# Two slots for filler work instead of one in a fused attention and feed-forward kernel

## The reference

```python
xn = layernorm(x)                      # x: (2, 8192, 1024)
latent = xn @ Wc_down                  # 1024 -> 512
q = latent @ Wq_up                     # 16 heads of 64
k, v = split(latent @ Wkv_up)          # one k, one v of 64 for all heads
y = softmax(causal(q k^T / 8)) v
s = y @ Wc_proj
gate = xn @ (w_gate/127).T; up = xn @ (w_up/127).T     # 1024 -> 3072
ffn = (silu(gate) * up) @ (w_down/127).T
out = x + s * silu(ffn)
```

## Time and profile before

| | us |
|---|---|
| median of the runs (2 runs, 3533.99 to 3546.13) | 3540.06 |
| the profiled execution | 3540.48 |
| its span, slowest core (core 0) | 3538.0 |
| spans of the other seven cores | 3485.8 to 3526.6 |
| TensorE busy | 2251.4 (64%) |
| ScalarE busy | 1336.4 (38%) |
| VectorE busy | 1189.5 (34%) |
| GpSimd busy | 413.1 (12%) |

### The profile page before, as it was taken

The page is one execution under the profiler, slowest core; times in us unless marked ns, Lnnn a source line. Parts: engine busy times, 40 slices in busy tenths (PEclk is TensorE's granted clock), DMA queues, the critical chain, the costliest instruction groups (busy, mean ns, idle before and its releaser), DMA issues.

```text
span 3538.0 us, 34007 instructions; the slowest of 8 cores (3485.8 to 3538.0 us)
## 1 busy us (share of the span) xinstructions
PE 2251.4 (64%) x10552; PEld 1056.5 (30%) x10592; DVE 1189.5 (34%) x2154; ACT 1336.4 (38%) x1489; POOL 413.1 (12%) x329
## 2 busy tenths in 40 slices
PE   1334546455574685584757748598576798488886
PEld 1212223222241252252224322252222442223422
DVE  3545342432423334424243241422322321411221
ACT  0112222221331343232534437344455436375355
POOL 0100212123042100100000000000000000000000
PEclk7556767676696796796869968677676787687878
DMA  5000539548193271461006300063000251011500
GB/s 94 32 33 32 66 63 120 92 78 154 23 110 73 36 169 51 104 153 65 32 14 134 112 21 25 14 150 96 14 17 26 65 141 43 15 31 45 141 26 13
DMA packets 549452, 240.57 MB, mean 68 GB/s; under 512 B 476576, under 2 KB 532896, under 8 KB 549280
## 3 DMA queue, kind: packets, MB, share of 16 engines
q1 hardware_dynamic: 431952, 195.27, 20.9%
q0 software_dynamic: 117328, 43.14, 11.3%
HBM read 250.00 MB, written 27.26 MB: 78 GB/s over the span
## 4 chain that ended last, share of the span: by engine, by line
PE 39%; DVE 20%; DMA 16%; issue 11%; ACT 10%; POOL 4%; DVEq 1%; SPq 0%; ACTq 0%; POOLq 0%
PE ps_y L548 10%; PE ps_sc L561 9%; ACT p_sb L572 7%; PE ps_u L717 5%; PE ps_u L724 4%; PE ps_u L788 3%; POOL p_sb L580 3%; DVE recbf L600 3%; DMA wd_t<-wdbf 3%; DMA wu_t<-wu 3%; PE ps_u L638 2%; DVE stat L299 2%; DMA wd_t<-wd 2%; DMA xt<-xb 2%; DVE xnT L371 2%
## 5 line engine op out<-in xcount | busy, mean ns | idle before, releaser
L572 ACT ACTIVATE p_sb<-ps_sc 128x1024 bf16<-128x1024 f32 x1088 | 1099.9, 1023 | 1483.0 <-PE ps_sc L561 1465.9
L548 PE MATMUL ps_y<-p_sb,vaug_sb 128*65 128x512 bf16 x2176 | 773.2, 442 | 236.9 <-POOL p_sb L580 147.3
L561 PE MATMUL ps_sc<-qs,kT_sb 65*128 65x512 bf16 x2176 | 774.3, 443 | 20.0 <-DVE qs L529 20.0
L580 POOL TENSOR_TENSOR p_sb<-p_sb,masks_sb 128x1024 bf16<-128x1024 bf16 x128 | 273.1, 2143 | 2698.2 <-ACT p_sb L572 2698.0
L548 PEld LDWEIGHTS ps_y<-p_sb,vaug_sb 128*65 128x65 bf16 x2176 | 218.7, 123 | 693.6 <-issue 628.7
L788 PE MATMUL ps_u<-wd_t,h_sb 128*128 128x512 bf16 x744 | 234.6, 444 | 140.7 <-DMA wd_t<-wd 59.0
L561 PEld LDWEIGHTS ps_sc<-qs,kT_sb 65*128 65x128 bf16 x2176 | 227.2, 110 | 245.8 <-issue 138.2
L717 PE MATMUL ps_u<-xnT_own,wg_t 128*128 128x256 bf16 x1536 | 228.3, 299 | 97.5 <-DVE h_sb L735 55.1
L590 DVE CAST yf<-ps_y 64x1024 bf16<-64x1024 f32 x32 | 38.8, 1213 | 617.7 <-PE ps_y L548 617.7
L364 PE MATMUL ps_u<-ident_sb,xn_t 128*128 128x128 bf16 x640 | 81.0, 269 | 259.5 <-DVE xn_t L329 225.7
L724 PE MATMUL ps_u<-xnT_own,wu_t 128*128 128x256 bf16 x1536 | 229.3, 299 | 21.5 <-DMA wu_t<-wu 21.3
(11 more groups left out here) (88 smaller groups left out, 1391.7 us busy)
## 6 DMA issues: line engine op xcount, KB each, us to landing
wg_t<-wgbf SPq DMA_DIRECT2D x144, 256.0 KB, 3.5
wu_t<-wubf SPq DMA_DIRECT2D x144, 256.0 KB, 3.7
wd_t<-wdbf SPq DMA_DIRECT2D x288, 128.0 KB, 2.2
xt<-xb SPq DMA_DIRECT2D x64, 512.0 KB, 4.6
xo_t<-xo SPq DMA_DIRECT2D x32, 512.0 KB, 3.9
wg_t<-wg POOLq DMA_DIRECT2D x48, 256.0 KB, 9.0
wu_t<-wu POOLq DMA_DIRECT2D x48, 256.0 KB, 8.9
wd_t<-wd POOLq DMA_DIRECT2D x96, 128.0 KB, 3.9
```

Source lines behind the costliest of these rows:

```text
L548: last = O("tensor", lambda e_, t=t, nh=nh, par=par: e_.matmul(ps_y[0:65, nh * 512:(nh + 1) * 512], vaug_sb[:, t, :], p_sb[:, par, nh * 51 ...
L561: sct = O("tensor", lambda e_, t=t, nh=nh, sb2=sb2: e_.matmul(ps_sc[:, sb2 * 1024 + nh * 512:sb2 * 1024 + (nh + 1) * 512], kT_sb[0:65, t * ...
L572: ex = O("scalar", lambda e_, sb2=sb2: e_.activation(p_sb[:, sb2, :], ps_sc[:, sb2 * 1024:(sb2 + 1) * 1024], AF.Exp), [sct, st["p_war"][sb ...
L580: mtoks[t] = O("gpsimd", lambda e_, pview=pview, mj=mj: e_.tensor_tensor(pview, pview, masks_sb[:, mj, :].unsqueeze(1).broadcast_to([128, ...
```

## The change

The one variable becomes two: act_m for a must or epilogue generator, act_l for a lazy one. A pump first goes on with act_m. If there is none, it advances lazy work when nothing of tq_must or of the ready epiq is pending, and also at every third pump when something is. Only then does it start an entry of tq_must or epiq. So a feed-forward piece stands at every third pump between must generators, though never inside one, and ready epilogues come ahead of lazy work. A lazy generator that stalls uses its pump up.

The core of the diff (the two draining loops after it replace `park_or_finish` by `finish_must` and active by act_l in the same manner):

```diff
--- before.py
+++ after.py
@@ -851,7 +851,8 @@
         tq_must = deque()
         tq_lazy = deque()
         epiq = deque()
-        active = [None]
+        act_m = [None]
+        act_l = [None]
         tick = [0]
         EPI_DELAY = 6
 
@@ -875,40 +876,38 @@
                     return "stall"
             return "active"
 
-        def start_item(item, lazy=False):
-            r = item()
-            if r is None:
-                return
-            if adv(r, 1, tq_lazy) == "active":
-                active[0] = (r, lazy)
-
-        def park_or_finish():
-            a = active[0]
-            if a is None:
-                return
-            if a[1]:
-                tq_lazy.appendleft(a[0])
-            else:
-                for _ in a[0]:
+        def finish_must():
+            if act_m[0] is not None:
+                for _ in act_m[0]:
                     pass
-            active[0] = None
-
-        def lazy_step_force():
-            a = active[0]
-            if a is not None and a[1]:
-                if adv(a[0], 1, tq_lazy) != "active":
-                    active[0] = None
-                return
+                act_m[0] = None
+
+        def lazy_step():
+            if act_l[0] is not None:
+                r = adv(act_l[0], LAZY_STEPS)
+                if r == "stall":
+                    tq_lazy.appendleft(act_l[0])
+                    act_l[0] = None
+                elif r == "done":
+                    act_l[0] = None
+                return True
             if tq_lazy:
                 ent = tq_lazy.popleft()
                 if callable(ent):
                     ent = ent()
                     if ent is None:
-                        return
-                if adv(ent, 1, tq_lazy) == "active":
-                    active[0] = (ent, True)
-                return
-            raise RuntimeError("stalled with no lazy work")
+                        return True
+                r = adv(ent, 1)
+                if r == "active":
+                    act_l[0] = ent
+                elif r == "stall":
+                    tq_lazy.appendleft(ent)
+                return True
+            return False
+
+        def lazy_step_force():
+            if not lazy_step():
+                raise RuntimeError("stalled with no lazy work")
 
         def enqueue_group(g):
             def own_item(g=g):
@@ -931,20 +930,20 @@
             tick[0] += 1
             if vecq:
                 vecq.popleft()()
-            a = active[0]
-            if a is not None:
-                g, lz = a
-                if lz and tq_must:
-                    tq_lazy.appendleft(g)
-                    active[0] = None
-                else:
-                    r = adv(g, LAZY_STEPS if lz else 1, tq_lazy)
-                    if r != "active":
-                        active[0] = None
-                    if r != "stall":
-                        return
+            if act_m[0] is not None:
+                if adv(act_m[0], 1) != "active":
+                    act_m[0] = None
+                return
+            must_pending = bool(tq_must) or (bool(epiq) and
+                                             tick[0] >= epiq[0][0])
+            if (act_l[0] is not None or tq_lazy) and \
+                    (tick[0] % 3 == 0 or not must_pending):
+                lazy_step()
+                return
             if tq_must:
-                start_item(tq_must.popleft())
+                r = tq_must.popleft()()
+                if r is not None and adv(r, 1) == "active":
+                    act_m[0] = r
                 return
             if epiq and tick[0] >= epiq[0][0]:
                 rdy, ent = epiq.popleft()
@@ -954,21 +953,17 @@
                     return
                 r = adv(ent, 1)
                 if r == "active":
-                    active[0] = (ent, False)
+                    act_m[0] = ent
                     return
                 if r != "stall":
                     return
                 epiq.appendleft((rdy, ent))
-            if tq_lazy:
-                ent = tq_lazy.popleft()
-                if callable(ent):
-                    start_item(ent, lazy=True)
-                else:
-                    if adv(ent, LAZY_STEPS, tq_lazy) == "active":
-                        active[0] = (ent, True)
+                lazy_step()
+                return
+            lazy_step()
 
         def drain(q):
-            park_or_finish()
+            finish_must()
             while q:
                 run_all(q.popleft())
```

More of the change, by code:

```diff
@@ L1024, in build_program @@
                     lazy_step_force()
-        while tq_lazy or active[0] is not None:
-            a = active[0]
+        while tq_lazy or act_l[0] is not None:
+            a = act_l[0]
             if a is not None:
-                for _ in a[0]:
+                for _ in a:
                     pass
-                active[0] = None
+                act_l[0] = None
                 continue
```

## The result

The changed kernel takes **3446.6 us**, the median of 11 runs (3433 to 3484). The kernel before took 3513.1 us, the median of 10 runs, and the ratio is 0.9796 with a 95% interval of 0.9765 to 0.9828. (Medians are of all runs; ratios are of mean times, without the single runs in which one die ran at a lower clock and took longer.) That is 2.0% faster; whether it is a little under or over 2% the interval leaves open. The forecast was 3525, within a range of 3460 to 3590.

The account below looks back on a forecast made before the run. The prediction saw no engine full and the time as a sum of waits along TensorE's queue. Its terms, +32 - 46 - 12 - 19 + 34 - 14 + 10 = -15, taken from 3540.5, gave 3525 us, range 3460 to 3590.

Parts of the forecast that it names:

- (a): Slot starts: pieces put there take the cover of other waits and delay L460 and L475; +32 us, bounds +10 and +55.
- (e): SyncE's queue: loads and the DMA into yT wait behind first-pass write-backs in slots 1 to 3; +34 us.
- the rival that was given 0.05: Slot starts: the clock stays up, L460 and L475 run at 1.95 us in every slot; 52 us less, 3473, chance 0.05.
- Both stay: Slots 3 and 4: the own tile's load still waits behind a write-back, as before; VectorE sat 6.37 us for it.
- (b): First pass, gate/up: thirteen pieces stand apart with must work between, hiding weight transfers; -46 us, bounds -70 and -15.
- (c): First pass, down: three of 8 pieces stand apart and find four of six tiles loaded; -12 us, bounds -30 and 0.
- (d): Second pass and pass starts: five gate/up pieces stand apart, slot 7's new pass starts under a wait; -19 us.
- (g): Masks: mask multiplies in bare steps lose or gain the cover of pieces in slots 5 to 7; net +10 us.
- (f): Projection: a piece or bare step fills its wait behind the epilogue, partly lost to ps_u; -14 us, bounds -25 and 0.
- Waits absorb the pieces: First head groups ahead of the projection: about 50 pieces cost 1 us instead of 2.99; -100, 3440, chance 0.13.
- SyncE's order decides: First pass: thirteen lone pieces hold SyncE's queue and delay loads, 130 us in place of 34; 3620, chance 0.10.
- The pieces run cold: The 50 pieces run at the lower clock level, 1.7 us more each; +85, 3610, chance 0.06.

Follow-up runs that it names:

- e1: The changed kernel without the third-pump rule, lazy work only when nothing else is pending, epilogues still ahead of it: 3528.2 us, ratio 1.0021 to the kernel before.
- e9: The changed kernel with no third pump in slots 0 and 1: 3459.1 us, ratio 0.9815 to the kernel before.
- e5: The kernel before, with feed-forward weights cast to bf16 by twelve HBM-to-HBM DMAs at the program's start, no write-backs: 3396.5 us, ratio 0.9616.
- e6: The changed kernel with feed-forward weights cast to bf16 by twelve HBM-to-HBM DMAs at the program's start, no write-backs: 3387.1 us, ratio 0.9594.
- e7: The changed kernel with no lazy piece while the projection is the next epilogue entry: 3474.7 us, ratio 0.9846 to the kernel before.
- e4: The changed kernel with the third-pump rule barred in each slot's first five pumps: 3454.3 us, ratio 0.9816 to the kernel before.
- e8: The changed kernel with third pumps barred in a slot's first five pumps once the first pass is through: 3453.6 us, ratio 0.9788 to the kernel before.
- e11: The kernel with the HBM-to-HBM casts delayed until slot 0's values are done, no third pump, one lazy piece ahead of each projection: 3402.5 us, ratio 0.9657.

## Why the prediction was wrong

Its direction was right by sign only: 15 us faster, and on core 7 it was 72. By its own terms, on that core:

**(a), slot starts: +32 predicted, or +46 with slot 1's part of (e), which can't be parted from it; -3 measured for both. This is the step that failed.** The measure is the time from a slot's start to the end of the step with the queries, less 2.99 us for each piece and 1.15 for each bare step drawn in. Slots 2, 3, 5, 6, 9 and 11 were put at +1.8 each, 10.8 together, and came to -10.7 (-8.4, -4.1, -0.3, +0.9, +0.4, +0.8). Slots 1, 4, 7 and 13 were put at 21.2 and came to +13.1 (+10.6, -2.9, +5.8, -0.4). Slot 10 was put at +3.9, it is +1.1. Slots 8, 12 and 14 were put at -3.6, they are -6.5. The delays came about as described: in slot 9 L460 begins 13.0 us later, as forecast, and L475 4.1. What failed is their price. First, L460 and L475 were put at the lower level, 3.57 us, in every slot. But L475 now follows L460 by 0.94 us and keeps the higher level that L460, or the piece before it, has brought back: in 7 of the 15 slot starts it takes 1.95 us, in the others 3.25 to 3.57. This is the rival that was given 0.05, half true. I argued against it with L475's 9 us wait, and that wait was the very one which (a) itself moved ahead of L460. By the Trainium skill's page "TensorE: Matmul & The Clock Gate" (Part 1) sustained work restores the rate, and these rows agree; I had applied the page's rule to the idle time and not to L460's work. In slot 13 both run in 1.95 us, and the slot's loss over the pieces is nothing instead of 5.3:

```profile
2676.57 1.86 PE L717 MATMUL ps_u<-xnT_own,wg_t 128*128 128x256 bf16 x8 [15.93 <-DVE xnT_own L371]
...
2681.41 1.95 PE L460 MATMUL ps_u<-xnT_own,wc_sb 128*128 128x128 bf16 x32
2684.30 1.95 PE L475 MATMUL ps_u<-latT,wq_sb 128*128 128x128 bf16 x32 [0.94 <-DVE latT L468]
```

Second, slots 2 and 3 start earlier than before, for reasons that are not the matmuls'. Slot 3's is the load of xo_t, next. Slot 2's is bookkeeping. There VectorE's first reduction of the own tile stood behind a reciprocal, before:

```profile
303.74 6.54 DVE L600 RECIPROCAL recbf<-rec 1x1024 bf16<-1x1024 f32 x1
310.31 1.22 DVE L299 TENSOR_REDUCE stat<-xo_t 128x1 f32<-128x1024 f32 x1
```

and after:

```profile
310.99 6.54 DVE L600 RECIPROCAL recbf<-rec 1x1024 bf16<-1x1024 f32 x1
317.57 0.42 DVE L406 CAST kT_sb<-ps_u 64x256 bf16<-64x256 f32 x1
```

Slot 2 starts at 302.30 us before and at 329.48 after. The third pumps have pushed slot 1's last keys past its end, and the reciprocal now stands ahead of them in slot 1's last step. So slot 2's first step fell from 16.4 to 8.6 us, and slot 1's last one rose from 9.9 to 27.2, with a piece in it. In e1, where epilogues also go first but no third pump is taken, slot 2's first step is 16.4 us as before. Without these 8.4 us of slot 2 the measure of (a) is +5, still far from +46.

**(e), SyncE's queue: slot 1's 14 us are 10.6 by the measure of (a), which holds both terms there** (it waits 9.22 for the load). "Both stay" was wrong. VectorE's waits for the own tile at slots 3 and 4 were 9.68 and 7.04 us on core 7 and are 2.73 and 5.02: between the slot's start and the load four write-backs are issued before and two now. The time to the end of the step with the own tile's first transposes fell from 24.7 to 18.0 in slot 3, and in slot 4 from 24.6 to 23.9 with a piece in it. All its waits for xt grew only from 35.4 to 53.2 us. The sign for slot 1 was right and its price of no use, as e9 shows: barring slot 1 wins nothing, because its pieces return in slot 4's run.

**(b), (c), (d), (g) and the rest of (e): -47 predicted, about -57 measured**, the remainder of core 7's 72 us (-65 if slot 2's 8.4 us are not given to (a)). They were not measured one by one, so that the sum came near says little of each. The run in slot 3 is 20 us shorter with four pieces fewer, in the way of (b). The steps with the first pass's eight down pieces sum to 88.2 us against 89.5, but three of them now also hold waits of must work, so (c) can't be read from that. e5 and e6 show that the class is right: without the casts the change wins nothing in slots 0 to 7.

**(f), the projection: -14 predicted, -13 measured** by the rows; e7 gives 19 in all. I let a third of the piece be lost to ps_u. In slots 7, 9, 11 and 13 it is absorbed almost whole, because L638's wait for the DMA and the lower clock of its first two pieces vanish behind it. In slot 6 the piece costs 3 us over its own, which was not foreseen.

**The base: 27 us.** 3540.5 us at the measured ratio is 3468, within the range given. A look at the other die would have shown core 0's lower clock, with 46 us more than core 7 in slots 11 to 15. How much of the 27 us it explains is not shown; beside the experiments the kernel before had medians of 3522.5 to 3527.5.

**The rivals.** "Waits absorb the pieces" named the right time, 3440, but by luck: e4 and e8 show that the pieces at the slot starts bring nothing, and only those at the projection are absorbed. "SyncE's order decides" was wrong, its cost is slot 1's 10.6 us, of which the starts of slots 3 and 4 give 7 back. "The pieces run cold" is real and small: L717 and L724 together are busy 458.1 us instead of 430.8, 27 us where the rival had 85, and L460, L475 and L638 give 29.6 of it back.

## What to carry to other kernels

When a piece of work is put in front of a wait, price the matmuls behind it at the clock they will then have, and follow the first waits of each slot back to the queue that causes them: here two write-backs fewer ahead of a load took 7 us off slot 3's first wait, more than any piece that was moved is worth. See also whether work that left a slot's start has only gone into the step before it, as the reciprocal did. Read the idle time of the group ahead together with that of the group which you freed, since 245 us that left four groups were 60 us of time. And before reordering work around slow transfers, measure the kernel without them: the copies ahead of the first slot gave 135 us, and with them there the new order gave 8, which can't be told from nothing.

## What the runs showed of the hardware that was not expected

- The same program ran 35 us apart on two cores whose granted clock was 0.750 and 0.792, in one execution; from slot 11 on a gate/up step was 3.17 us on the one, at a granted clock of 0.81, and 2.99 on the other, at 1.00.
- L475's 32 matmuls took 1.95 us after L460 had run 3.35 us, though L460 itself had begun at the lower level after 2.79 us of waiting: the clock rose within L460's 32 matmuls.
- In e5, from 10 to 230 us, with the twelve HBM-to-HBM casting copies of 1536 KB, the DMA engines of core 7 were nine tenths busy or more at 103 to 208 GB/s; a copy landed 106 to 202 us after its issue (medians of the three weights). Beside them a 512 KB load landed in 11.9 us, and in e11, where they run in slot 1, in 30.6 us there. In e5 they still beat 256 KB casts with write-backs by 135 us over the run.
